# Maxima as exponential biases, and expert results scattered straight to tokens, in a two-layer decoder kernel

## What is computed

```python
# cross-attention of layer 1: 64 context and 64 own tokens, 128 keys, 16 heads of width 8
p = softmax((q @ k.T) * 8 ** -0.5); r = p @ v; x = norm(x + r @ Wproj + b)
# the block's own attention: 64 keys, 16 heads of width 8, same softmax
x1 = norm(x + attention(x)) * g1 + be1
# second mixture: 8 experts, top 2 of the gate, gates sum to 1
p, e = top_k(softmax(x1 @ Wg + bg), 2); p = p / p.sum()
y = sum_k p[k] * (gelu(x1 @ W1[e[k]] + b1[e[k]]) @ W2[e[k]] + b2[e[k]])
out = norm(x + norm(x1 + y) * g2 + be2)        # the last two norms of the kernel
```

## Time and profile before

| What | Value |
|---|---|
| median of 3 runs | 1700.76 us |
| profiled execution, its span | 1700.69 us, 1698.9 us |
| TensorE busy | 1376.5 us (81%) |
| VectorE busy | 1166.6 us (69%) |
| ScalarE busy | 872.7 us (51%) |
| GpSimd busy | 642.1 us (38%) |
| stage 1, about | 0 to 475 us |
| stage 2, about | 475 to 1372 us |
| between stages 2 and 3 | 1372 to 1402 us |
| stage 3, about | 1402 to 1567 us |
| stage 4, about | 1567 to 1699 us |

### The profile page before, as it was taken

One profiled execution on the slowest core, in us unless ns is written; L12 is line 12 of the kernel. 1 busy time (PEld: TensorE's weight loads), 2 busy tenths in 40 slices (PEclk: granted clock), 3 DMA queues, 4 the chain that ended last, 5 costly groups with the idle time before them and its releaser, 6 DMA issues.

```text
span 1698.9 us, 46753 instructions
## 1 busy us (share of the span) xinstructions
PE 1376.5 (81%) x19192; PEld 1120.8 (66%) x19192; DVE 1166.6 (69%) x3279; ACT 872.7 (51%) x2058; POOL 642.1 (38%) x912
## 2 busy tenths in 40 slices
PE   6899999999859988988989899898997739998000
PEld 5788787888737766766767667676675528887000
DVE  4777887778666888877878787888887631100565
ACT  3556555665425765556566565665666514444000
POOL 6415335243052245433443525535223220000885
PEclk8899999999979999999999999999999959999555
DMA  9932221211110011000010100101000026665232
GB/s 342 381 99 73 66 69 59 87 58 40 61 50 8 9 27 38 25 22 13 24 33 12 40 11 24 36 12 30 21 8 27 14 93 202 202 202 154 62 90 71
DMA packets 114293, 123.04 MB, mean 72 GB/s; under 512 B 21920, under 2 KB 87456, under 8 KB 113824
## 3 DMA queue, kind: packets, MB, share of 16 engines
q1 hardware_dynamic: 107936, 107.46, 19.6%
q0 software_dynamic: 6144, 12.60, 2.6%
HBM read 65.49 MB, written 54.53 MB: 71 GB/s over the span
## 4 chain that ended last, share of the span: by engine, by line
PE 53%; DVE 24%; POOL 8%; ACT 7%; issue 5%; DMA 1%; SPq 1%; DVEq 0%; POOLq 0%; ACTq 0%
PE bank L1847 6%; PE bank L1714 5%; DVE P L1492 4%; PE bank L2101 4%; DVE gs L1491 4%; PE bank L2094 3%; POOL P L1046 3%; PE bank L1726 3%; PE bank L1699 3%; PE bank L1896 2%; PE bank L1970 2%; PE bank L1885 2%; PE bank L1935 2%; PE bank L1892 2%; PE bank L1908 2%
## 5 line engine op out<-in xcount | busy, mean ns | idle before, releaser
L1166 ACT ACTIVATE P<-P 128x512 f32<-128x512 f32 x256 | 160.1, 630 | 99.9 <-DVE P L1492 98.5
L1491 DVE TENSOR_REDUCE gs<-bank 128x8 f32<-128x512 f32 (+1 forms) x256 | 174.5, 682 | 43.2 <-PE bank L1699 21.3
L1714 PE MATMUL bank<-const,P 128*128 128x128 f32 x1152 | 177.2, 284 | 29.4 <-ACT P L1166 20.8
L1492 DVE TENSOR_TENSOR P<-bank,gs 128x512 f32<-128x512 f32 x256 | 177.1, 692 | 8.8
L1714 PEld LDWEIGHTS bank<-const,P 128*128 128x128 f32 x1152 | 130.5, 143 | 70.0 <-ACT P L1166 42.1
L1847 PE MATMUL bank<-XT,wb 128*128 128x256 f32 x512 | 138.2, 397 | 3.1 <-ACT PT L1077 1.2
L1046 POOL DMA_INDIRECT P<-rows_x,places x64 | 64.6, 1009 | 200.9 <-DMA rows_x<-R 183.4
L1172 ACT ACTIVATE PT<-bank 128x512 f32<-128x512 f32 x192 | 109.7, 594 | 51.1 <-PE bank L1714 49.8
L1649 DVE TENSOR_TENSOR R<-bank,Q 128x256 f32<-128x256 f32 x40 | 17.0, 425 | 164.0 <-PE bank L2101 164.0
L989 POOL TENSOR_TENSOR P<-P,gs 128x512 f32<-128x512 f32 x64 | 66.0, 1046 | 155.4 <-DVE gs L1528 154.9
L1263 ACT ACTIVATE PT<-bank,Q 128x256 f32<-128x256 f32 x160 | 67.4, 471 | 84.7 <-PE bank L2094 84.4
(11 more groups left out here) (264 smaller groups left out, 3564.5 us busy)
## 6 DMA issues: line engine op xcount, KB each, us to landing
Q<-in_wm SPq DMA_DIRECT2D x40, 578.0 KB, 3.8
rows_x<-blank SPq DMA_DIRECT2D x4, 4864.0 KB, 33.7
y_mid<-PT SPq DMA_DIRECT2D x16, 512.0 KB, 2.8
y_mid<-D SPq DMA_DIRECT2D x16, 512.0 KB, 2.8
X<-rows_x SPq DMA_DIRECT2D x40, 128.0 KB, 2.2
rows_x<-R SPq DMA_DIRECT2D x40, 128.0 KB, 2.6
wb<-in_wb SPq DMA_DIRECT2D x1, 4228.0 KB, 15.3
V<-in_ctxT SPq DMA_DIRECT2D x32, 128.0 KB, 3.0
```

Of the source, the lines that this page charges most:

```text
L1166: act.activation(P[s][:, i, :], P[s][:, i, :], ACT.Exp, scale=scale).then_inc(p.of(s), 1)
L1491: st2(dve.tensor_reduce(mx, v, AX.X, ALU.max))
L1492: dve.tensor_tensor(P[s][:, i, :].rearrange("p (g m) -> p g m", m=width), v, each(mx, width), ALU.subtract).then_inc(s_sub.of(s), 1)
L1714: last = pe.transpose(tile(banks[s][i], t), tile(P[s][:, i, :], t), ident)
```

## The change

1. **Biases.** In the 128-key attention VectorE takes only a minimum over negated scores (the factor -(8 ** -0.5) now sits in the constant `quad`, which the queries are multiplied by). The subtraction is gone: ScalarE exponentiates each group of 128 keys by itself, straight out of PSUM, with scale -1 and the minimum as bias: four instructions of 128x128 for one of 128x512. The 64-key `fs` attention keeps its two steps, with a minimum and a scale of -1 in place of a maximum and 8 ** -0.5. `as` stays.
2. **Rows that carry their token.** A row of `rows_x` grows from 128 to 132 floats: the x1 row, token number + 1, first expert, and the two gates. `place` writes these four into the new buffer `XW` (X1 is a view of it); `blank`, which clears `rows_x`, is wider too. The weights get one more column, the expert's number.
3. **Stage 3 scatters.** A new step `tp` on VectorE (eight instructions on 128x2) works out, for each row of a tile, its gate and its row in a new tensor `y_rows` (first expert's result in one part, second expert's in the other, blank rows to spare rows). After b2 is added VectorE multiplies the tile by the gates, and GpSimd scatters it (two indirect DMAs per tile). SyncE's write is gone.
4. **Stage 4.** The four gathers per group become two plain loads of `y_rows` by SyncE. GpSimd adds the two results, VectorE adds x1, forms (R - mean) * g2 and then times the root plus x, with one pair of instructions each; the last normalization moves to ScalarE with a shift that GpSimd works out in two more small instructions.
5. **Orders.** All lists of `ORDERS` are written anew, and `pool3` and `act4` are added.

```diff
-                      ("tile", TILES), ("rowbase", 32))
+                      ("tile", TILES), ("rowbase", 32), ("spare", TILES * T))
-        X1 = per_slot("X1", [128, T, DIM])
+        XW = per_slot("XW", [128, T, WIDE])
+        X1 = [XW[s][:, :, 0:DIM] for s in range(SLOTS)]
...
@@ SyncE, stage 3 @@
             def tile(j, s):
                 yield "tx"
                 if j:
                     sp.wait_ge(m_x_ps.of(s), m_x_ps.at(j - 1, s))
+                    sp.wait_ge(m_row.of(s), m_row.at(j - 1, s))
...
-                yield "ty"
-                sp.wait_ge(m_y.of(s), m_y.at(j, s))
-                to = sp.value_load(table[0:1, j * SLOTS + s, 0:1], min_val=0, max_val=XROWS - NT)
-                sp.dma_start(d["rows_x"][bass.ds(to, NT), :].rearrange("(t p) d -> p t d", p=128), R[s][:, :, :]).then_inc(tile_y[s], 16)
+            for s in range(SLOTS):
+                sp.wait_ge(m_gelu.of(s), m_gelu.at(ROUNDS - 1, s))
+                sp.wait_ge(tile_y[s], 16 * T * ROUNDS)
+            for s in range(SLOTS):
+                load_results(0, s)
@@ SyncE, stage 4 @@
+                if n + 1 < passes:
+                    yield "ly"
+                    sp.wait_ge(c_ln_mv.of(s), c_ln_mv.at(n, s))
+                    load_results(n + 1, s)
+                    load_last_x1(n + 1, s)
+                    yield "lx"
+                    sp.wait_ge(c_r2_mv.of(s), c_r2_mv.at(n, s))
+                    load_last_x(n + 1, s)
@@ GpSimd @@
+            def tile(j, s):
+                yield "sc"
+                pool.wait_ge(m_gated.of(s), m_gated.at(j, s))
+                for t in range(T):
+                    pool.indirect_dma_start(d["y_rows"][:, :], bass.IndirectOffsetOnAxis(
+                        ap=gidx[s][:, t, j % 2:j % 2 + 1], axis=0), R[s][:, t, :], None).then_inc(tile_y[s], 16)
...
+                yield "su"
+                pool.wait_ge(last_y[s], 16 * 3 * (n + 1))
                 if n:
                     pool.wait_ge(c_ln_mv.of(s), c_ln_mv.at(n - 1, s))
-                for t in range(T):
-                    for k in range(2):
-                        pool.indirect_dma_start(P4[s][:, k, 128 * t:128 * t + 128], None, d["rows_x"][:, :], bass.IndirectOffsetOnAxis(
-                            ap=places[:, (n * SLOTS + s) * T + t, k:k + 1], axis=0)).then_inc(gathered[s], 16)
+                pool.tensor_tensor(P4[s][:, 2, :], P4[s][:, 0, :], P4[s][:, 1, :], ALU.add).then_inc(c_sum.of(s), 1)
@@ ScalarE @@
+            def exps_of_negated(n, s, stage, use):
+                for i in range(BANKS):
+                    yield part_of(stage, i)
+                    act.wait_ge(b_s_sub.of(s), b_s_sub.at(n, s, i + 1, use=use))
+                    for g in range(4):
+                        ins = act.activation(P[s][:, i, 128 * g:128 * g + 128], banks[s][i][:, 128 * g:128 * g + 128], ACT.Exp,
+                                             bias=gs[s][:, 0, 4 * i + g:4 * i + g + 1], scale=-1.0)
+                    ins.then_inc(b_p.of(s), 1)
@@ VectorE @@
+            def least_of_negated(n, s, stage, use):
+                for i in range(BANKS):
+                    yield part_of(stage, i)
+                    dve.wait_ge(b_s_ps.of(s), b_s_ps.at(n, s, i + 1, use=use))
+                    dve.tensor_reduce(gs[s][:, 0, 4 * i:4 * i + 4], banks[s][i][:, :].rearrange("p (g m) -> p g m", m=128), AX.X,
+                                      ALU.min).then_inc(b_s_sub.of(s), 1)
...
             def tile(j, s):
+                yield "tp"
+                dve.wait_ge(tile_x[s], 16 * (j + 1))
+                dve.wait_ge(tile_w[s], 16 * (j + 1))
...
                 yield "ty"
                 dve.wait_ge(m_down_ps.of(s), m_down_ps.at(j, s))
                 if j:
-                    dve.wait_ge(tile_y[s], 16 * j)
+                    dve.wait_ge(tile_y[s], 16 * T * j)
                 dve.tensor_tensor(R[s][:, :, :], tok(half(s, 0)), over(part(wm[s], WM, "b2"), T), ALU.add).then_inc(m_y.of(s), 1)
+                dve.wait_ge(m_y.of(s), m_y.at(j, s))
+                for t in range(T):
+                    ins = dve.tensor_scalar(R[s][:, t, :], R[s][:, t, :], small[s][:, 3, t:t + 1], None, ALU.mult)
+                ins.then_inc(m_gated.of(s), 1)
```

More of the change, by code:

```diff
@@ L651, in build @@
         last_x = [sem(f"last_x{s}") for s in range(SLOTS)]
-        gathered = [sem(f"gathered{s}") for s in range(SLOTS)]
+        last_y = [sem(f"last_y{s}") for s in range(SLOTS)]
         written = [sem(f"written{s}") for s in range(SLOTS)]
@@ L662, in build @@
         m_gelu = m_act("gelu")
+        m_row = m_dve("row")
         m_y = m_dve("y")
+        m_gated = m_dve("gated")
         c_ln_mv = c_dve("ln_mv")
         c_r2_mv = c_dve("r2_mv")
-        c_out = c_dve("out")
+        c_act = Lane(act_did, C_ACT, m_act.after + m_act.total * ROUNDS)
+        c_out = c_act("out")
+        c_sum = c_pool("sum")
         c_ln_rstd = c_pool("ln_rstd")
@@ L1050, in gather @@
                 yield "n5"
[L1051 to L1053 removed]
+                pool.wait_ge(c_r2_mv.of(s), c_r2_mv.at(n, s))
+                apart(pool)
+                pool2(pool, pool.tensor_scalar(rstd[s][:, :], mv[s][:, :, 1], EPS, None, ALU.add))
+                pool2(pool, pool.tensor_tensor(rstd[s][:, :], rstd[s][:, :], power[:, 0:T], ALU.pow))
+                pool2(pool, pool.tensor_tensor(shift[s][:, :], mv[s][:, :, 0], rstd[s][:, :], ALU.mult))
+                pool.tensor_scalar(shift[s][:, :], shift[s][:, :], -1.0, None, ALU.mult).then_inc(c_ln_rstd.of(s), 1)
+            in_turn(pool, ORDERS["pool4"], [finish(n, s) for n in range(passes) for s in range(SLOTS)])
         @block.scalar
@@ L1265, in _, with finish @@
             in_turn(act, ORDERS["act3"], [tile(j, s) for j in range(ROUNDS) for s in range(SLOTS)])
+            def finish(n, s):
+                yield "n5"
+                act.wait_ge(c_ln_rstd.of(s), c_ln_rstd.at(n, s, use=1))
+                if n:
+                    act.wait_ge(written[s], 16 * n)
+                for t in range(T):
+                    last = act.activation(X1[s][:, t, :], R[s][:, t, :], ACT.Identity, bias=shift[s][:, t:t + 1], scale=rstd[s][:, t:t + 1])
+                last.then_inc(c_out.of(s), 1)
+            in_turn(act, ORDERS["act4"], [finish(n, s) for n in range(passes) for s in range(SLOTS)])
         @block.vector
```

168 lines of the change are left out of this document (92 added, 76 removed), and 466 rows, old and new, of tables (act1, act2, act3, dve1).

## The result

The changed kernel takes 1596.17 us (median of 4 runs, 1594.56 to 1599.2), the kernel before 1702.17 us in the 4 runs beside it (1695.51 to 1703.92). The profiled execution of after has a span of 1597.4 us against 1698.9: 101.5 us less.

A forecast was written before the change was run, and what follows sets the result against it. TensorE was taken to bound stages 2 and 3, GpSimd's queue stage 4. The span, 1698.9 - 52 + 2 - 8 = 1640.9 us, plus 1.8 us outside it gave 1643 us; range 1616 to 1674 us.

The forecast's parts named there:

- Stage 4, -52: Stage 4: replacing GpSimd's gathers by plain loads takes it from 114 to 62 us, -52 us.
- The level pair of engines: Stage 4: GpSimd and VectorE come out level at 3.5 us a group, 56 us for 16 groups.
- The way from stage 3 to 4: From VectorE's last b2 addition to its first stage 4 step: 9.5 us for 9.8, no change, 0 to +3.
- Stage 3, +2: Stage 3: +3 us at the start from SyncE's row loads, steady state 4.1 us a tile; +2, bounds -4 to +10.
- Stage 2, -8: Stage 2: levelling VectorE and ScalarE saves a tenth of TensorE's 75 idle us in the middle, -8, bounds -30 to +30.
- The price of four exponentials: Stage 2, ScalarE: four 128x128 exponentials take 1.33 us for one of 0.630, +89 us in all, bounds +40 to +148.
- Stage 1, 0: Stage 1 keeps its work, only its lists differ and the blank transfer is 3% longer: 0, bounds -6 to +6.
- bound by its loads: Rival, stage 4: SyncE's five DMAs a group make about 5 us a group, 80 us not 60; 1663 us, chance 0.13.
- upper price: Rival, stage 2: ScalarE becomes second bound at 0.46 us more per bank, +30 instead of -8; 1681 us, chance 0.08.
- The slower case by `tp`: Rival, stage 3: late weights park VectorE in `tp`, delaying b2 additions, 2 us a tile; 1723 us, chance 0.04.
- the case of no effect: Rival, stage 4: gathers are bound by row traffic and plain loads are as slow; 1700 us, chance 0.03.
- Stage 2 gains more: Rival, stage 2: nearly half of TensorE's middle idle time goes, -30; 1621 us, chance 0.12.

The follow-up runs named there:

- the two additions: Changed kernel with one more unread 128x256 addition per group in stage 4: on GpSimd 1604.78 us, in a separate run on VectorE 1600.89 us.
- the next relief: One-exponential kernel in the new lists, given one minimum or negated maximum per 512-score row as bias, no subtraction in any bank: 1570.43 us.
- one exponential in the new lists: Changed kernel with one 128x512 exponential per bank, using the first group's minimum for all four groups, in place of four: 1578.86 us.

## Why the prediction was wrong, point by point

**What bounds the kernel.** Stages 2 and 4 were read rightly. For stage 3 I wrote that TensorE is busy 156 of 165 us, hence 4.1 us a tile. That reading failed. The products of stage 3, from the groups by shape, before and then after:

```profile
L2094 PE MATMUL bank<-XT,Q 128*128 128x256 f32 x320 | 85.8, 388 | 2.6 <-DMA Q<-in_wm 1.6 <-ACT XT L1259 0.8
L2101 PE MATMUL bank<-Q,PT 128*128 128x128 f32 x640 | 85.7, 280 | 6.6 <-ACT PT L1263 5.8
```

```profile
L2181 PE MATMUL bank<-XT,Q 128*128 128x256 f32 x320 | 87.5, 387 | 1.1 <-ACT XT L1314 0.8 <-DMA Q<-in_wm 0.2
L2188 PE MATMUL bank<-Q,PT 128*128 128x128 f32 x640 | 83.7, 276 | 0.0
```

The same 960 products, 171 us by these rows either time, fit into 165 us before and into 149.4 after. Their records overlap: one starts while the last still drains. So a busy share of 95% still had 15 us to give. It stood on the page of before, in the row of the weight loads (16.0 us idle ahead of them, 14.1 of it until gelu), and the prediction doesn't use it:

```profile
L2101 PEld LDWEIGHTS bank<-Q,PT 128*128 128x128 f32 x640 | 79.7, 191 | 16.0 <-ACT PT L1263 14.1
```

The weight loads' busy time in the earlier trace rows was 137.5 of 165 us, 83%. After it is 139.6 of 153, 91%. The Trainium skill (Perfetto Trace Analysis, Identifying the Most-Contended Engine) warns of this: the matmul busy share isn't a good measure of how near TensorE is to its roofline, and the share of the peak flops and the busy share of LDWEIGHTS are to be used instead. The traces agree (matmuls 95% busy and weight loads 83% before, with 15 us to give), and the prediction didn't draw on it.

**Stage 4, -52.** Right: -51.4, and for the reason given, since the gathers put back cost 58 us. From VectorE's first step to its last 60 us were forecast and 61.6 measured (1524.85 to 1586.47), 3.85 a group. The level pair of engines is borne out by the two additions. One sign did not come: between their first and last steps VectorE is busy 82% and GpSimd 77%, not 85 to 90%.

**The way from stage 3 to 4.** 9.5 us forecast for 9.8 (its terms add up to 9.7), measured 8.4.

**Stage 3, +2.** The start is right (+3 forecast, +4.0 measured), and the cause also: with SyncE's new order the way took 15.7 us among the old operations and 15.5 with the old lists of TensorE and ScalarE, against 11.9. `tp` did no harm: VectorE waits 21.3 us for weights in after, 15.9 of them once, at the start, and no wait of TensorE in stage 3 is ended by VectorE. The steady state is the step that failed, "TensorE still at 4.1 us a tile". I costed two new lists at nothing because TensorE seemed to be full; taken out again they cost 15.3 us.

**Stage 2, -8.** The failed step is the sentence that takes a tenth of TensorE's idle time for levelling. It is a guess without a row behind it, and it gives the order of the work no price, while the change writes every list anew. In the old lists the relief gave 8.3 us and relief and split together lost 11; in the new ones the relief gave 76.0. That the old-list 8.3 is near the forecast's 8 is luck, since the forecast's 8 holds the split as well. The bound of -30 was 10 us short, as it was drawn from TensorE's idle time alone: the waits fell by 31.0, and the busy time of the same 13378 matmuls fell too, from 785 to 775 us, with 26.4 us less at 1.2 GHz.

**The price of four exponentials.** Mis-sized: 1.33 us forecast, 1.11 measured; +61 us for ScalarE rather than +89. VectorE's side was right: 85 us less forecast, 85.4 measured. "Nothing" on the path was wrong too: the split costs 19.5 us there. The 1.27 us worked out in the prediction from the Trainium skill (ScalarE: Activation LUTs, What ACT_TABLE_LOAD costs) was nearer than mine, and the trace is below it too.

**Stage 1, 0.** +1.7 measured, within the bounds and no more than single executions differ by.

**The rivals.** Stage 4 is not bound by its loads, which hold GpSimd up for 4.5 us in all. ScalarE didn't come to its upper price. The slower case by `tp` and the case of no effect fell. "Stage 2 gains more" had the right sign and the right stage, with too low a bound. No rival said that the lists themselves are an edit with a price, in two stages at once.

## What to carry to other kernels

When a change rewrites the order of the work as well as the work, the two have no prices of their own: one relief was worth 8 us in one order and 76 in another, so a forecast needs a case for the order, as wide as the waits it could remove. Look for those waits on the weight loads as well as on the products: in stage 3 the weight loads waited 14.1 us for gelu where the products showed 5.8. Add what the clock can give back: time at the lower clock in the kernel before, halved, is a bound for it. And once an order fits its operations, the next relief may give little (8.6 us for 72), so measure it before building on the last rate.

## What the runs showed of the hardware

- 128x128 exponentials from PSUM with a bias per partition last 393 ns by the record but advance by 0.25 us from start to start in a row (after, the eight from 800.86 us take 2.18 us). One of 128x512 with such a bias takes 689 ns, and from SBUF without one 639.
- Nearly the same matmuls show less busy time when they follow each other without gaps, since their records then overlap more: 160.8 us of 169 in stage 3 before, 152.0 of 153 in after, both at a mean granted clock of 0.99.
- Between the two ends of stage 2 TensorE's clock fell to 1.2 GHz ten times in before, three times in after, and once with one exponential in the new lists. The lower the waits, the fewer the falls, in these three.
- Stage 3 moved 216 GB/s in after against 194 before, with the DMA engines busy 0.72 and not 0.63, and the up-products' weight loads waited for the weights' DMA 1.9 us in all.
